# The two split layers of an attention and feed-forward kernel keep their results in PSUM, and every engine gets a new order of work

## The reference

```
y   = routed experts(x) + shared expert         # 8 experts of 64, two chosen for each token; leaky gate * up, then down
q, k, v = split(y @ W_qkv + b_qkv)
x1  = x + layernorm((q k^T / scale * band) v)    # band of 32, "ln1"
xn  = layernorm(x1)                              # "ln2"
Q   = xn @ Wq (16 heads of 64);  k, v = xn @ Wkv (one head for all);  Q and k normalized
a   = softmax(8 Q k^T + position bias, mask)     # 129 keys: 128 and a null key
z   = layernorm((a v) @ Wout)                    # "ln3"
h   = silu(z @ w1) * (z @ w2)                    # "l1", 128 -> 512
h   = gelu(h @ h1);  h = gelu(h @ h2)            # "l2", "l3", 512 -> 512
out = x1 + h @ w3                                # "l4", 512 -> 128
```

## Time and profile before

| | |
|---|---|
| median of 3 runs | 853.04 us (852.45 to 853.72) |
| the profiled execution | 853.67 us, its span in the trace 851.9 us |
| PE busy | 800.9 us, 94% of the span |
| DVE busy | 589.0 us, 69% |
| ACT busy | 603.0 us, 71% |
| POOL busy | 447.4 us, 53% |
| mean granted TensorE clock | 0.992 of full speed |
| DMA | 16.98 MB in all, 20 GB/s on average |

### The profile page before, as it was taken

How to read it: one execution, slowest core, us unless ns; L and a number is a source line. 1 busy time by engine, 2 the same in 40 slices (tenths; PEclk the granted TensorE clock), 3 DMA queues, 4 the chain that set the end, 5 groups by cost and what they waited for, 6 DMA issues and landing times. The chain is left out here.

```text
span 851.9 us, 16700 instructions
## 1 busy us (share of the span) xinstructions
PE 800.9 (94%) x5368; PEld 599.7 (70%) x5368; DVE 589.0 (69%) x1581; ACT 603.0 (71%) x1649; POOL 447.4 (53%) x388
## 2 busy tenths in 40 slices
PE   5978879999999999999999999999999989999987
PEld 4756556678676777678676777778776766777777
DVE  5578878776767686776767586776767786664522
ACT  2314768588857888588866878588866978779944
POOL 3027874754558365754558364654558455944200
PEclk9989999999999999999999999999999999999999
DMA  7041100000010000100010000100010000000000
GB/s 245 1 156 35 63 14 4 2 2 2 1 41 2 1 2 2 42 1 2 2 42 1 2 1 2 41 1 1 1 42 1 2 1 2 13 2 1 13 7 7
DMA packets 15588, 16.98 MB, mean 20 GB/s; under 512 B 1408, under 2 KB 13072, under 8 KB 15120
## 3 DMA queue, kind: packets, MB, share of 16 engines
q1 hardware_dynamic: 15216, 15.27, 5.7%
q10 hardware_dynamic: 288, 0.66, 0.2%
HBM read 13.81 MB, written 2.11 MB: 19 GB/s over the span
## 5 line engine op out<-in xcount | busy, mean ns | idle before, releaser
L632 POOL TENSOR_TENSOR sb_sm<-sb_sm,sb_rden 128x512 f32<-128x512 f32 x128 | 135.9, 1068 | 209.0 <-DVE sb_rden L1097 209.0
L728 ACT ACTIVATE sb_sm<-sb_sm,sb_nmx 128x129 f32<-128x129 f32 x512 | 199.2, 393 | 26.7 <-DVE sb_nmx L1092 26.4
L1084 DVE SCALAR_TENSOR_TENSOR sb_sm<-ps_S,sb_rq,sb_biasm 128x129 f32<-128x129 f32 x512 | 140.9, 343 | 60.2 <-PE ps_S L1316 21.2
L625 POOL TENSOR_TENSOR sb_biasm<-sb_bias,sb_maskn 128x512 f32<-128x512 f32 x128 | 165.8, 1310 | 21.5 <-DVE sb_sm L1084 12.8
L615 POOL TENSOR_TENSOR sb_rq<-sb_qss,sb_mhalf 128x16 f32<-128x16 f32 x32 | 92.5, 2916 | 41.5 <-DVE sb_qss L1069 41.5
L728 ACT ACTIVATION_READ_ACCUMULATOR sb_sm<-sb_sm,sb_nmx 128x1 f32 x512 | 97.1, 190 | 0.0
L1316 PEld LDWEIGHTS ps_S<-sb_k,sb_qs 64*128 64x128 f32 x1024 | 64.8, 187 | 34.7 <-issue 32.9
L1316 PE MATMUL ps_S<-sb_k,sb_qs 64*128 64x129 f32 x1024 | 83.1, 291 | 6.5 <-DVE sb_sm L1084 6.5
L1092 DVE TENSOR_REDUCE sb_nmx<-sb_sm 128x4 f32<-128x516 f32 x128 | 85.8, 675 | 0.6
L735 ACT ACTIVATE sb_pT<-ps_T 128x512 f32<-128x512 f32 x128 | 75.0, 591 | 14.3 <-PE ps_T L1324 14.3
L1324 PE MATMUL ps_T<-sb_ident,sb_sm 128*128 128x128 f32 x512 | 76.8, 276 | 3.4 <-ACT sb_pT L735 2.4
(11 more groups left out here) (226 smaller groups left out, 1800.7 us busy)
## 6 DMA issues: line engine op xcount, KB each, us to landing
sb_xg<-in_xT SPq DMA_DIRECT2D x8, 256.0 KB, 4.2
...
```

Source lines behind the costliest of these rows:

```text
L625: pool.tensor_tensor(biasm[:, heads, 1:NK], bias0[:, heads], maskn[:, j // 4].unsqueeze(1).broadcast_to([128, 4, S]), ALU.add)\
L632: pool.tensor_tensor(sm[:, heads, 1:NK], sm[:, heads, 1:NK], rden[:, heads].unsqueeze(2).broadcast_to([128, 4, S]), ALU.mult)\
L728: ins = act.activation(sm[:, h], sm[:, h], ACT.Exp, bias=nmx[:, h:h + 1], accum_out=den[:, h:h + 1])
L1084: ins = dve.scalar_tensor_tensor(sm[:, h], bank(g, "sim", n, odd)[:, m * NK:(m + 1) * NK], rq[:, k * HEADS + h:k * HEADS + h + 1], biasm[: ...
```

## The change

1. `gated` writes its result back into the PSUM bank of its second operand, and the high and low parts of `l1` are made from there; `gelu2` writes into the bank that it reads, and the parts of `l2` are made from there. `al` holds only the silu. In exchange each such bank is free for its next writer only when the low part has been made. Silu no longer waits for the low part of the block before but for its gated product, and gelu no longer waits for the low part of the block before.
2. Stage A of group 0 uses a ring F of four banks: the three of M and one bank of T.
3. `condT`, `wgT` and `wt` are fetched on ACT's queue, `wg` and `wu` on SP's right behind the first `x`. POOL sets `eps` first, and ACT does a small Copy at once, before its first real instruction, so that its first load of function tables is done then.
4. All tables of `ORDER` are new. The first half of the last group keeps only `l3d.0-1` in the pass `last`; its `l3` blocks 2 and 3 and its `l4` move to the pass `drain`, among the second half's `zT` and `l1`.

The core of the diff (of the tables only the lines whose rows are not shown further below):

```diff
     "pe drain": """
-        zT.0 l1.0-3 l2.0-3 l3.0-3 l4.0
+        l3p.2 zT.0 l3p.3 l1.0 l4p.0 l1.1-3 l2.0-3 l3.0-3 l4.0
...
     "dve start": """
-        rw.0 xl.0 sim.0 max.0 sim.1 exp.0 max.1 inv.0 exp.1 sim.2 exp.2 inv.1 max.2 exp.3 sim.3 inv.2 max.3-4
-        exp.4 inv.3 pl.4 sim.4 max.5 down.0 inv.4 sim.5 max.6 qkv.0 scores.0 inv.5 max.7 inv.6 mix.0 sim.6 max.8
...
+        rw.0 xl.0 sim.0 max.0 sim.1 exp.0 max.1 inv.0 exp.1 max.2 sim.2 inv.1 exp.2 inv.2 max.3 exp.3 sim.3
+        exp.4 inv.3 sim.4 max.4-5 pl.4 inv.4 max.6 inv.5 down.0 sim.5 inv.6 max.7 qkv.0 sim.6 inv.7 scores.0
...
+RINGS = {ring: [(ring, i) for i in range(n)] for ring, n in BANKS.items()}
+RINGS["F"] = RINGS["M"] + [("T", 1)]
...
+def uses(step, g, k):
...
-    return "MM" if (step, k) == ("exp", NX - 1) else USES.get(step, "")
+    rings = "MM" if (step, k) == ("exp", NX - 1) else USES.get(step, "")
+    return rings.replace("M", "F") if g == 0 and STAGE[step] == "A" else rings
...
-            DRAINED |= {("l1", o, 0): (silued, o + 1), ("l1", o, 1): (l1_gated, o + 1),
-                        ("l2", o, 0): (l2_gelu, o + 1), ("l3", o, 0): (l3_ready, o + 1)}
+            DRAINED |= {("l1", o, 0): (silued, o + 1), ("l1", o, 1): (l1_ready, o + 1),
+                        ("l2", o, 0): (l2_ready, o + 1), ("l3", o, 0): (l3_ready, o + 1)}
...
+            act.wait_ge(first_const, 1)
+            act.activation(idle_act[:], eps[:, 0:1], ACT.Copy)
...
             def silu(g, o):
                 act.wait_ge(l1_psum.sem, l1_psum.at(g, 2 * o + 1))
-                act.wait_ge(l1_ready.sem, l1_ready.at(g, max(o - 1, 0)))
-                act.wait_ge(l2_ready.sem, l2_ready.at(g, 0))
+                act.wait_ge(l1_gated.sem, l1_gated.at(g, max(o - 1, 0)))
...
-                act.activation(hAs[0][:, o, t], al[:, o % 2, t], ACT.Copy).then_inc(l1_high.sem, 1)
+                act.activation(hAs[0][:, o, t], bank(g, "l1", o, 1)[:, t], ACT.Copy).then_inc(l1_high.sem, 1)
...
             def gelu2(g, o):
                 act.wait_ge(l2_psum.sem, l2_psum.at(g, o + 1))
-                act.wait_ge(l2_ready.sem, l2_ready.at(g, max(o - 1, 0)))
                 t = tokens(g)
-                act.activation(al[:, o % 2, t], bank(g, "l2", o)[:, t], ACT.Gelu, scale=h1s[:, o:o + 1]).then_inc(l2_gelu.sem, 1)
+                act.activation(bank(g, "l2", o)[:, t], bank(g, "l2", o)[:, t], ACT.Gelu, scale=h1s[:, o:o + 1])\
+                    .then_inc(l2_gelu.sem, 1)
...
-                dve.scalar_tensor_tensor(al[:, o % 2, t], bank(g, "l1", o, 1)[:, t], w2s[:, o:o + 1], al[:, o % 2, t],
+                dve.scalar_tensor_tensor(bank(g, "l1", o, 1)[:, t], bank(g, "l1", o, 1)[:, t], w2s[:, o:o + 1], al[:, o % 2, t],
                                          ALU.mult, ALU.mult).then_inc(l1_gated.sem, 1)
...
-                low(hAs[1][:, o, t], al[:, o % 2, t], hAs[0][:, o, t], None, l1_ready)
+                low(hAs[1][:, o, t], bank(g, "l1", o, 1)[:, t], hAs[0][:, o, t], None, l1_ready)
```

More of the change, by code:

```diff
@@ L120 @@
+        q.5 ssq.0 kT.0 ssc.0 vs.0 q.6-7
     """,
     "dve start": """
-        rw.0 xl.0 sim.0 max.0 sim.1 exp.0 max.1 inv.0 exp.1 sim.2 exp.2 inv.1 max.2 exp.3 sim.3 inv.2 max.3-4
-        exp.4 inv.3 pl.4 sim.4 max.5 down.0 inv.4 sim.5 max.6 qkv.0 scores.0 inv.5 max.7 inv.6 mix.0 sim.6 max.8
-        inv.7 sim.7 max.9 inv.8 ln1.0 inv.9 sim.8 max.10 ln2.0 max.11 inv.10 sim.9 xnT.0 sim.10 inv.11 max.12
-        maskn.0 q.0 max.13 q.1 inv.12 max.14 sim.11 q.2 kv.0 max.15 inv.13 q.3 inv.14 q.4-5 inv.15 kT.0 pl.5
@@ L126 @@
-        q.6-7 ssq.0 ssc.0 vs.0
+        rw.0 xl.0 sim.0 max.0 sim.1 exp.0 max.1 inv.0 exp.1 max.2 sim.2 inv.1 exp.2 inv.2 max.3 exp.3 sim.3
+        exp.4 inv.3 sim.4 max.4-5 pl.4 inv.4 max.6 inv.5 down.0 sim.5 inv.6 max.7 qkv.0 sim.6 inv.7 scores.0
+        max.8 sim.7 max.9 mix.0 max.10 inv.8-9 ln1.0 sim.8 max.11 ln2.0 inv.10 sim.9 inv.11 xnT.0 max.12 sim.10
+        max.13 kv.0 inv.12 maskn.0 q.0-1 max.14 q.2 sim.11 inv.13 max.15 q.3 inv.14 q.4 inv.15 kT.0 q.5-6 ssq.0
+        pl.5 ssc.0 vs.0 q.7
@@ L134 @@
+        zl.0 inv.2 qkv.0 sim.3 l1.0 inv.3 max.4 h1.0 l1.1 h1.1 sim.4 l1.2 h1.2 max.5 l1.3 sim.5 inv.4 h1.3
+        scores.0 max.6-7 inv.5 sim.6 inv.6 h2.0 inv.7 h2.1 max.8 h2.2-3 mix.0 sim.7 max.9 inv.8 max.10 sim.8
+        inv.9 ln1.0 inv.10 max.11 ln2.0 inv.11 sim.9 xnT.0 max.12 sim.10 kv.0 max.13 sim.11 max.14 q.0 inv.12
+        max.15 q.1-2 kT.0 inv.13-14 l4.0 maskn.0 q.3 inv.15 q.4-5 ssq.0 q.6 ssc.0 vs.0 q.7
     """,
     "dve seventh": """
-        rw.0 xl.0 ln3.0 sim.0 exp.0 max.0 exp.1 sim.1 exp.2 max.1 exp.3-4 inv.0 max.2 sim.2 max.3 inv.1-2 zT.0
@@ L137 @@
[L137 to L140 removed]
+        rw.0 xl.0 ln3.0 exp.0 sim.0 exp.1-2 sim.1 max.0 exp.3 max.1 sim.2 inv.0 max.2 exp.4 inv.1 zT.0 max.3
@@ L141 @@
+        down.0 inv.2 zl.0 qkv.0 l1.0 sim.3 h1.0 l1.1 max.4 inv.3 h1.1 l1.2 sim.4 h1.2 l1.3 max.5 sim.5 inv.4
+        scores.0 h1.3 max.6-7 inv.5-6 sim.6 max.8 mix.0 inv.7 sim.7 inv.8 max.9 ln1.0 sim.8 h2.0 max.10 ln2.0
+        max.11 inv.9-10 h2.1 xnT.0 sim.9 max.12 inv.11 h2.2 sim.10 max.13 h2.3 inv.12-13 kv.0 max.14 q.0-1
+        sim.11 q.2 max.15 q.3 maskn.0 inv.14 kT.0 inv.15 q.4-6 ssq.0 ssc.0 q.7 vs.0
     """,
     "dve last": """
-        sim.0 max.0 sim.1 ln3.0 max.1 inv.0 max.2 sim.2 inv.1 max.3 zT.0 l4p.0 zl.0 inv.2 sim.3 l1.0-1 h1.0
@@ L148 @@
+        sim.8 max.9 inv.8 h2.3 max.10-11 inv.9-11 sim.9 max.12 sim.10 max.13 ln3d.0 max.14 inv.12 zTd.0 inv.13
+        zld.0 l4.0 l1d.0 h1d.0 l1d.1 h1d.1 sim.11 inv.14 l1d.2-3 h1d.2-3 max.15 inv.15 h2d.0-3
     """,
     "dve drain": """
-        ln3.0 zT.0 zl.0 l1.0 h1.0 l1.1-2 h1.1 l1.3 h1.2-3 h2.0-3 l4.0
+        ln3.0 zT.0 zl.0 l1.0 h1.0 l4p.0 l1.1-2 h1.1-2 l1.3 h1.3 h2.0-3 l4.0
     """,
     "pool fill": """
-        pb.0 nk.0 nb.0 pb.1 ln1.0 xb.0 ln2.0 bias+.0-2 kv.0 bias+.3 qn.0-3
+        pb.0 nb.0 nk.0 pb.1 xb.0 ln1.0 ln2.0 bias+.0-3 kv.0 qn.0-3
```

149 lines of the change are left out of this document (69 added, 80 removed).

## The result

The changed kernel takes 822.6 us (median of 4 runs, 822.4 to 826.57) against 853.09 for the kernel before: a ratio of 0.9654, with a 95% interval of 0.9624 to 0.9684. The profiled execution took 822.41 us with a span of 820.6 and a mean granted clock of 0.998; the one of 826.57 had 0.991, so part of what separates executions is TensorE's clock.

The account below looks back on a forecast made before the run. TensorE, busy for 94% of the span, was taken as the bound. Fill -1.5, start -3, steady -6.5, seventh -1.5, last and drain -5 sum to -17.5 against 853.67: 836 us, range 826 to 848.

Parts of the forecast that it names:

- The new order puts that part behind `sim.4` and two `max` steps. That is -4.1: Start, DVE: moving a weight's low part removes `sim.5`'s 2.41 us wait and 1.7 lost at half clock; 1.1 given back.
- Start loses 9 instead of 3: Rival for a larger gain, 826 us: start loses 9, fill 3 and the end 7; chance 0.14.
- The fourth bank for first experts I cost at nothing: Fill: the extra bank wins 0, since the experts run back to back on TensorE there.
- The loads: Ahead of the first matmul: `condT` first on ACT's queue brings up to -1.5 us, -0.8 taken.
- The 6.9 us at half clock behind the table transfer stay: Fill: TensorE's 6.9 us at half clock behind the table transfer remain, so no gain there.
- Steady passes: Five steady passes: -1.7 us each at `xnT` and +0.4 each for held banks, -6.5 together.
- The term for `xnT`: Steady passes: with POOL idle during `ln2`'s norm, TensorE's wait at `xnT` goes, -1.7 us a pass.
- Held banks: `l1` in steady passes: banks wait for copy and low part, +0.4 us a pass (0 to 3); `l2` hidden.
- The low parts now read one operand from PSUM, so POOL cannot stretch them; that hides nothing on the path: Low parts on DVE: reading PSUM helps DVE but wins nothing on the path; no size given.
- slower: held banks in l1 and l2: Rival: waits on held banks at `l1`'s third and fourth block, 3.5 us a pass giving 858 us; chance 0.10.
- Tail: Last and drain: `l3` blocks fill TensorE's idle time behind `z.7`, no half clock; -5 us (-2 to -8).
- Table loads: ACT, steady passes: two more loads of 1.28 us each, taken as 0 because ACT has 23 us idle.

Follow-up runs that it names:

- before_pl4: The kernel before with one DVE step in start, the weight's low part `pl.4`, moved behind `sim.4` and `max.5`; 855.6 us.
- pl4_early: The changed kernel with the weight's low part `pl.4` back ahead of `sim.4` and the two `max` steps on DVE in start; 823.9 us.
- before_new_start: The kernel before with the new order in the pass start alone, on all engines; 848.4 us.
- old_loads: The changed kernel with `wt`, `wgT`, `condT` on SP's queue and `wg`, `wu` on ACT's again, early Copy kept; 825.7 us.
- old_fill: The changed kernel with the pass fill in the order of before on all engines; 827.8 us.
- hold_in_old: The kernel before with part 1 alone, and `l1`'s low parts moved up in DVE's steady order so that it can run; 867.1 us.
- psum_undone: The changed kernel with part 1 taken back: results in the SBUF buffer, old waits of silu and gelu, new orders kept; 849.2 us.
- old_steady_al: As psum_undone, with the five steady passes also in the order of before on all engines; 840.3 us.
- old_tail: The changed kernel with the passes last and drain in the order of before, held banks kept; 839.7 us.

## Why the prediction was wrong

The direction and most mechanisms were right, but every term was too small: the 13.8 us between the forecast sum and the spans are start 4.7, fill with the first matmul 4.4, steady and seventh 1.7 each, and last with drain 1.4. The two terms that failed in their reasoning are start and fill; behind them stands a price of part 1 with the wrong sign.

- **Start, the largest miss (-3 forecast, -7.7 measured).** The step that failed is "The new order puts that part behind `sim.4` and two `max` steps. That is -4.1". I read one wait of the earlier trace rows as if its owner were the cause. before_pl4 showed that the wait moves to another reader of DVE; pl4_early that it makes no difference in the new order. What counts is the sequence as a whole, 6.0 us, and then whether the clock falls (1.4 to 1.5 us for 3.4 us at 0.50). I did name "Start loses 9 instead of 3" as a rival, at 0.14 together with others. By the waits of before_new_start against those of the kernel before, the new order takes away 1.8 us at a `PT` that waited for an ACT copy, 1.6 us at a product that waited for DVE's line 949, 1.1 us at `xnT` and 1.9 of 5.7 us at `sim`, and adds 2.2 us at the `PT`s that wait for POOL's `pn` and 0.9 at a `sim`. Which of the many moves do that stays open; the two runs say only that `pl.4` is not it.
- **Fill (-1.5 with the first matmul, -5.9 measured).** The step that failed is "The fourth bank for first experts I cost at nothing". It is worth about 2 us with the new order, most of it as a fall of the clock that I did not foresee. The loads gave 1.3 by old_loads where I took 0.8. "The 6.9 us at half clock behind the table transfer stay" held for most kernels with the new fill (6.8 us in eight of them, 3.4 in the changed one and three others), but the stretch got shorter all the same: from the first matmul of the table to `xnT` it is 7.4 to 7.7 us in the kernels with the old front end and 5.2 to 5.9 in those with the new fill. The run old_fill, with the old order but the new loads and ring, has 6.2, so the order of fill has a part in it. The profiled execution lies at the favourable end, and that is luck: in the ten kernels with all of the new front end start begins at 72.1 to 74.2 us, 73.1 on average, and in the five with the old one at 77.6, so that 4.4 us is the typical gain.
- **Steady passes (-6.5 forecast, -8.2 measured).** The mechanism is right and shown three times: the norm takes 4.52 us with four POOL instructions beside it, 2.07 with one and 1.12 with none. The term for `xnT` was taken at 1.7 and gave 1.3 alone. Held banks, taken at +0.4 a pass, cost nothing (96.0 against 96.2 in hold_in_old).
- **Seventh (-1.5 forecast, -3.2 measured).** I took it like a steady pass. In psum_undone and old_steady_al, with the new order and the results in SBUF, it is 88.8, so 1.1 us are the order's and 2.1 the storage's. Four other kernels have 87.8 or 87.9: at the same code as here a `sim` waits 1.5 us in three of them where it waits 0.3 in the changed kernel.
- **Held banks.** "The low parts now read one operand from PSUM, so POOL cannot stretch them; that hides nothing on the path" is the step that hid the most (the full sentence allows that it "helps DVE"). It was true of the old order, where hardly a low part had POOL beside it. In the new one they do, and with both operands in SBUF they take 0.97 (`l1`) and 1.22 us (`l2`) at 512 columns instead of 0.69; that costs 2.6 to 2.8 us in each steady pass and 2.1 in the seventh. The total did not suffer from it, since the change does both, but I had the price of part 1 with the wrong sign. The rival "slower: held banks in l1 and l2" is real where the order does not fit (hold_in_old 15 us slower than the kernel before, old_tail 17 us slower than the changed one), and absent where it does.
- **Tail (-5 forecast, -6.4 measured).** Right in mechanism: no gap from `z.7` to `l1.0`, and full clock. But the order does it only with part 1, through the waits of gelu and silu that the description of the change lists and the sum leaves out.
- **Table loads.** Taken at nothing, and they are: ACT is busy 2.6 us more in a pass, and TensorE has no new wait in the steady passes. Of the 1380 ns for a drain that the Trainium skill (ScalarE: Activation LUTs, What ACT_TABLE_LOAD costs) adds, nothing shows here: in the earlier trace rows the exponential starts 0.01 us behind the load.

The Trainium skill (SBUF — State Buffer, Who interferes with whom) states the side of the rule that I passed over: a DVE instruction with at most one SBUF input, outside the two-port modes, does not contend with GpSimd. The trace agrees: 0.69 us from PSUM beside POOL, 1.72 a piece from SBUF.
